# Filler matmuls in the idle gaps of a recurrent loop, and its four gates on one set of partitions

## The reference, cut to what matters

```python
def step(carry, tgt):
    s, c, alpha = carry
    f = lax.conv_general_dilated(alpha, conv_w, (1,), 'SAME', ...)
    e = einsum('a,bta->bt', va, tanh(enc_proj + (s @ Wa_s.T)[:, None, :] + einsum('bft,af->bta', f, Wa_f) + ba))
    alpha_new = softmax(where(mask, e, -1e30), axis=1)[:, None, :]
    g = einsum('bt,btd->bd', alpha_new[:, 0], hbatch)
    y = ...
    rec = tgt @ L_ys.T + s @ L_ss.T + g @ L_gs_w.T + L_gs_b
    ig, fg, cg, og = split(rec, 4, axis=1)
    c_next = _sig(fg) * c + _sig(ig) * tanh(cg)
    s_next = _sig(og) * tanh(c_next)
```

## Time and profile before

| | us |
|---|---|
| median of three runs (lowest, highest) | 1775.82 (1774.48, 1776.86) |
| profiled execution, first to last instruction | 1777.0 |
| TensorE busy (matmul) | 1506.0, 85% |
| TensorE busy (weight load) | 1022.2, 58% |
| VectorE busy | 919.2, 52% |
| ScalarE busy | 528.9, 30% |
| GpSimd busy | 387.5, 22% |

### The profile page before, as it was taken

One profiled execution on the slowest core, in us unless ns is written; L12 is line 12 of the kernel. 1 busy time (PEld: TensorE's weight loads), 2 busy tenths in 40 slices (PEclk: granted clock), 3 DMA queues, 4 the chain that ended last, 5 costly groups with the idle time before them and its releaser, 6 DMA issues.

```text
span 1777.0 us, 43152 instructions
## 1 busy us (share of the span) xinstructions
PE 1506.0 (85%) x15683; PEld 1022.2 (58%) x15683; DVE 919.2 (52%) x4293; ACT 528.9 (30%) x2023; POOL 387.5 (22%) x1030
## 2 busy tenths in 40 slices
PE   6547999999888888888888888888888888887999
PEld 3334454544666666666666666666666666664443
DVE  4996643331555555555555555555555555553422
ACT  1342231221333333333333333333333333331211
POOL 3344321220000222222222222222222222222211
PEclk7658999999555555555555555555555555555999
DMA  8330000001200000000000000000000000000000
GB/s 326 141 115 11 1 1 0 1 1 52 77 0 0 0 0 0 0 0 0 0 0 0 0 0 0 0 0 0 0 0 0 0 0 0 0 0 1 1 24 25
DMA packets 17363, 34.51 MB, mean 19 GB/s; under 512 B 7476, under 2 KB 8675, under 8 KB 17332
## 3 DMA queue, kind: packets, MB, share of 16 engines
q1 hardware_dynamic: 17332, 34.10, 5.3%
HBM read 32.00 MB, written 2.10 MB: 19 GB/s over the span
## 4 chain that ended last, share of the span: by engine, by line
PE 62%; DVE 25%; issue 6%; ACT 5%; POOL 1%; DVEq 1%; SPq 1%; DMA 0%; POOLq 0%; ACTq 0%
PE bank L1243 18%; PE bank L1073 11%; PE bank L1193 6%; PE bank L1088 6%; PE bank L1221 5%; ACT eh L960 4%; DVE interT L746 4%; PE bank L1199 4%; DVE krep L764 3%; PE bank L1213 3%; DVE rinv L755 3%; DVE rs L743 2%; DVE g L760 2%; PE bank L1231 2%; DVE gat L771 2%
## 5 line engine op out<-in xcount | busy, mean ns | idle before, releaser
L1243 PE MATMUL bank<-krep,uh 128*128 128x128 f32 x1024 | 313.1, 461 | 23.6
L1243 PEld LDWEIGHTS bank<-krep,uh 128*128 128x128 f32 x1024 | 237.4, 320 | 92.4 <-DVE krep L764 92.4
L493 POOL TENSOR_TENSOR sscale<-ex,rinv 128x8 f32 x256 | 51.3, 200 | 667.6 <-DVE rinv L755 667.6
L1221 PE MATMUL bank<-eh,krep 128*128 128x4 f16 x2048 | 95.3, 168 | 92.5 <-ACT eh L960 92.5
L764 DVE TENSOR_TENSOR krep<-inv,ahn 128x128 f32<-128x128 f32 x512 | 162.2, 356 | 0.0
L1073 PE MATMUL bank<-xT,wbig 128*128 128x512 f16 x672 | 157.2, 386 | 3.7 <-DVE xT L591 3.7
L743 DVE TENSOR_TENSOR rs<-bank,rin 128x8 f32<-128x8 f32 x256 | 42.8, 167 | 198.1 <-PE bank L1199 198.1
L1221 PEld LDWEIGHTS bank<-eh,krep 128*128 128x128 f16 x2048 | 74.1, 105 | 114.0 <-ACT eh L960 114.0
L963 ACT ACTIVATE xs<-gat 64x8 f32<-64x8 f32 x256 | 53.4, 208 | 288.7 <-DVE gat L771 288.7
L955 ACT ACTIVATE interT<-bank 128x128 f16<-128x128 f32 x256 | 71.2, 278 | 216.9 <-PE bank L1193 216.9
L1181 PE MATMUL bank<-enc,identb 128*128 128x128 bf16 x771 | 128.4, 303 | 0.0
(11 more groups left out here) (201 smaller groups left out, 3044.5 us busy)
## 6 DMA issues: line engine op xcount, KB each, us to landing
wbig<-d_gate_qT SPq DMA_DIRECT2D x4, 896.0 KB, 10.1
wbig<-d_up_qT SPq DMA_DIRECT2D x4, 896.0 KB, 20.7
wbig<-d_down_qT SPq DMA_DIRECT2D x1, 3584.0 KB, 30.5
d_out<-x_sb SPq DMA_DIRECT2D x8, 256.0 KB, 2.0
sscale<-d_gate_sT SPq DMA_DIRECT2D x2, 896.0 KB, 8.6
interT<-d_gate_sT SPq DMA_DIRECT2D x2, 896.0 KB, 14.9
sscale<-d_up_sT SPq DMA_DIRECT2D x2, 896.0 KB, 4.2
interT<-d_up_sT SPq DMA_DIRECT2D x2, 896.0 KB, 4.3
```

What stands on the lines that cost most here:

```text
L1221: ins = mm(bank[4][:, 4 * gp:4 * gp + 4], hg2[:, j, h, gp * P:(gp + 1) * P], e[:, 4 * h:4 * h + 4], start=(first and gp == 0 and j == 0 an ...
L1243: mm(bank[1 - par][:, 0:P], uh[:, h, :], qv[:, h, :, :], start=False, stop=False, skip_group_check=True)
```

## The change

On ScalarE the two TanH of the gates become one over 16 columns of 64 partitions. For that VectorE writes `gat` as 64 x 16: two additions, each of 64 partitions, one of which takes its inputs from partitions 64 to 127. `xs` grows by the 8 columns that were `tfi`, and L778 reads them there.

The sum before the TanH now always lies in `bank[0]`. `bank[1]`, free by that, takes the results of matmuls that nothing reads. Sixteen of 512 columns stand between `down` and the loop. In each step `keep_busy(n)` issues a matmul of n columns (with `identb` as weights and 128 rows of the half-precision table `hg2` as the stream) ahead of TensorE's waits: 256 columns before that for `th_s`, 256 before `th_lo_ready`, 512 before `eh_ready`, 512 before `q0_ready`, and 512 and 256 behind L1243, ahead of the wait for the next `sh`. That is 2304 columns a step.

```diff
--- before.py
+++ after.py
@@ -162,14 +162,13 @@
         ex = sb("ex", [P, 2, 8])
         rinv = sb("rinv", [P, 2, B])
         g1 = sb("g1", [P, 8])
-        gat = sb("gat", [P, 8])
+        gat = sb("gat", [J, 16])
         rs = sb("rs", [P, 8])
         ahn = sb("ahn", [P, 8])
         sh = sb("sh", [J, B], F16)
         sl = sb("sl", [J, B], F16)
         qv = krep[:, 0, :, :].rearrange("p b t -> p (b t)").rearrange("p (i b t) -> p i b t", i=2, b=B)
-        tfi = sb("tfi", [J, 8])
-        xs = sb("xs", [J, 2, 12])
+        xs = sb("xs", [J, 2, 20])
         ab = sb("ab", [J, 8])
         tc_sb = sb("tc_sb", [J, B])
         s2 = sb("s2", [J, 2, B])
@@ -768,14 +767,15 @@
                     dve.wait_ge(s["ah_done"], l + 1)
                     nc.vector.tensor_tensor(by_half(ahn[:]), by_half(bank[7][:, 0:8]), norm, ALU.mult).then_inc(s["ahn_ready"], 1)
                     dve.wait_ge(s["prod_ready"], l + 1)
-                    nc.vector.tensor_tensor(gat[:], g1[:], rs[:], ALU.add).then_inc(s["g_ready"], 1)
+                    nc.vector.tensor_tensor(gat[:, 0:8], g1[J:P, :], rs[J:P, :], ALU.add)
+                    nc.vector.tensor_tensor(gat[:, 8:16], g1[0:J, :], rs[0:J, :], ALU.add).then_inc(s["g_ready"], 1)
                     dve.wait_ge(s["ahn_ready"], l + 1)
                     spread(0).then_inc(s["q0_ready"], 1)
                     dve.wait_ge(s["kept"], l + 1)
                     spread(1).then_inc(s["q1_ready"], 1)
 
                     dve.wait_ge(s["tg_ready"], l + 1)
-                    nc.vector.scalar_tensor_tensor(ab[:], tfi[:], 1.0, xs[:, par, 0:8], ALU.add, ALU.mult).then_inc(s["ab_ready"], 1)
+                    nc.vector.scalar_tensor_tensor(ab[:], xs[:, par, 12:20], 1.0, xs[:, par, 0:8], ALU.add, ALU.mult).then_inc(s["ab_ready"], 1)
                     dve.wait_ge(s["ab_ready"], l + 1)
                     nc.vector.scalar_tensor_tensor(xs[:, 1 - par, 0:4], ab[:, 0:4], 0.5, ab[:, 4:8], ALU.mult, ALU.add).then_inc(s["c_ready"], 1)
 
@@ -952,16 +952,15 @@
                 for par in range(2):
                     l = i * 2 + par
                     act.wait_ge(s["pre_done"], l + 1)
-                    nc.scalar.activation(th_hi, bank[par][:, 0:P], ACT.Tanh).then_inc(s["th_s"], 1)
-                    nc.scalar.activation(th, bank[par][:, 0:P], ACT.Tanh).then_inc(s["th_full"], 1)
+                    nc.scalar.activation(th_hi, bank[0][:, 0:P], ACT.Tanh).then_inc(s["th_s"], 1)
+                    nc.scalar.activation(th, bank[0][:, 0:P], ACT.Tanh).then_inc(s["th_full"], 1)
 
                     act.wait_ge(s["et_done"], l + 1)
                     act.wait_ge(s["mx_ready"], l + 1)
                     nc.scalar.activation(eh[:], bank[3][:, 0:8], ACT.Exp, bias=nmx[:, 0:1]).then_inc(s["eh_ready"], 1)
                     nc.scalar.activation(ex[:, par, :], bank[3][:, 0:8], ACT.Exp, bias=nmx[:, 0:1]).then_inc(s["ex_ready"], 1)
                     act.wait_ge(s["g_ready"], l + 1)
-                    nc.scalar.activation(xs[:, par, 4:12], gat[J:P, :], ACT.Tanh, scale=0.5)
-                    nc.scalar.activation(tfi[:], gat[0:J, :], ACT.Tanh, scale=0.5).then_inc(s["tg_ready"], 1)
+                    nc.scalar.activation(xs[:, par, 4:20], gat[:], ACT.Tanh, scale=0.5).then_inc(s["tg_ready"], 1)
                     act.wait_ge(s["c_ready"], l + 1)
                     nc.scalar.activation(tc_sb[:], xs[:, 1 - par, 0:4], ACT.Tanh, scale=0.5).then_inc(s["tc_ready"], 1)
 
@@ -1163,6 +1162,9 @@
                         pass
 
             down(2 * IT0, IT0, wd, B, last_gates)
+
+            for _ in range(16):
+                mm(bank[1][:], x_part[0][:, 0, 0:P], x_part[0][:, 0, :], start=True, stop=True)
             pe.wait_ge(s["setup_v"], 1)
             pe.wait_ge(s["mask_ready"], 1)
             pe.wait_ge(s["rin_ready"], 2 * B)
@@ -1175,13 +1177,17 @@
                 mm(bank[2][:, 0:T], bsel[:], maskb[:], start=True, stop=False, skip_group_check=True)
                 mm(bank[3][:, 0:8], etl[:], etr[:], start=True, stop=False, skip_group_check=True)
 
-            def context_part(par):
+            def context_part():
 
                 for j in range(3):
-                    mm(bank[par][:, 0:P], identb[:], enc3[:, j, :], start=(j == 0), stop=False, skip_group_check=True)
+                    mm(bank[0][:, 0:P], identb[:], enc3[:, j, :], start=(j == 0), stop=False, skip_group_check=True)
+
+            def keep_busy(n):
+
+                mm(bank[1][:, 0:n], identb[:], hg2[:, 0].rearrange("p h g -> p (h g)")[:, 0:n], start=True, stop=True)
 
             masks()
-            context_part(0)
+            context_part()
 
             with pe.Fori(0, S // 2) as i:
                 for par in range(2):
@@ -1190,7 +1196,7 @@
                     state_part = [(0, sh), (1, sh), (0, sl)]
                     for j, st in state_part:
                         pe.wait_ge(s["sl_ready" if st is sl else "sh_ready"], l + 1)
-                        last = mm(bank[par][:, 0:P], was2[:, j, :], st[:].unsqueeze(2).broadcast_to([J, B, TH]),
+                        last = mm(bank[0][:, 0:P], was2[:, j, :], st[:].unsqueeze(2).broadcast_to([J, B, TH]),
                                   start=False, stop=(st is sl), skip_group_check=True)
                     last.then_inc(s["pre_done"], 1)
 
@@ -1200,6 +1206,7 @@
                                       start=(j == 0 and st is sh), stop=(j == 1 and st is sl))
                     last.then_inc(s["sp_done"], 1)
 
+                    keep_busy(256)
                     pe.wait_ge(s["th_s"], l + 1)
                     for b in range(B):
                         for h in range(2):
@@ -1209,9 +1216,11 @@
 
                     for j in range(2):
                         mm(bank[3][:, 0:8], th_hi, vae2[:, j, :], start=False, stop=False, skip_group_check=True)
+                    keep_busy(256)
                     pe.wait_ge(s["th_lo_ready"], l + 1)
                     mm(bank[3][:, 0:8], th_lo, vae2[:, 0, :], start=False, stop=True, skip_group_check=True).then_inc(s["et_done"], 1)
 
+                    keep_busy(512)
                     pe.wait_ge(s["eh_ready"], l + 1)
 
                     def gates(parts, e, first, final):
@@ -1236,11 +1245,14 @@
                         mm(bank[7][:, 0:8], fwd[:, j, :], eh[:], start=(j == 0), stop=False)
                     mm(bank[7][:, 0:8], fwd[:, 0, :], el[:], start=False, stop=True).then_inc(s["ah_done"], 1)
                     masks()
-                    context_part(1 - par)
+                    context_part()
+                    keep_busy(512)
 
                     for h in range(2):
                         pe.wait_ge(s[f"q{h}_ready"], l + 1)
-                        mm(bank[1 - par][:, 0:P], uh[:, h, :], qv[:, h, :, :], start=False, stop=False, skip_group_check=True)
+                        mm(bank[0][:, 0:P], uh[:, h, :], qv[:, h, :, :], start=False, stop=False, skip_group_check=True)
+                    keep_busy(512)
+                    keep_busy(256)
 
 
             pe.wait_ge(s["hist_done"], S)
```

## The result

| | before | after |
|---|---|---|
| median of four runs, us (lowest, highest) | 1775.15 (1773.78, 1776.86) | 2050.67 (2049.64, 2050.69) |
| profiled execution's span, us | 1777.0 | 2048.9 |
| TensorE busy (matmul) | 85% | 95% |
| first and last `rinv` of the loop, us | 447.6, 1601.6 | 447.7, 1873.9 |

A forecast was written before the change was run, and what follows sets the result against it. Taken as bound by the gate path, then L1193, TanH, score and exponentials. Swinging clock: loop (-12.8 + 156)/2 = +72, burst +2.2, behind the loop -0.9, so +73: 1850 on the profiled 1777.0, median 1849 us; range 1778 to 1930.

The forecast's parts named there:

- For 64 partitions as for 128: VectorE's second add ahead of the spreads: costs 0.08 us, the same for 64 partitions as for 128.
- So a step is bound by the gate path: Loop step: `gat`, two TanH, `ab`, `sh`, then L1193 bound it; L1243's 1.22 us is not the bound.
- L1193 waits for `sh` all the same: State's matmul in the loop: `sh` sets its start, so L1243's own gain at 2.4 GHz is off the path.
- The merged TanH gives nothing back where the spreads hide it: Gates: `ab` queues behind the spreads, +0.07 us in 224 steps, -0.09 in the first 32; together +12.8 us.
- One bank, 0: L1181's bank was read by L955/L956 half a step before, so nothing waits; cost 0.
- The 2304 columns: Unread matmuls in each step: cost 0 at 2.4 GHz, +0.61 us at 1.2, second add's 0.08 included.
- Each level leads to the other: Loop's clock: up, it falls; down, gaps close and it rises; half the steps at each level, +72 us.
- Down for good, 1934: Rival for the loop's clock: the first fall is never undone, 1777 + 158 - 1 = 1934 us; chance 0.10.
- Held up all the way, 1763: Rival: burst carries the clock into the loop, filled gaps keep it up, 1763 us; chance 0.18.
- The -0.10 a step for the higher clock: Loop at 2.4 GHz: L1193 -0.08 and L1213 with similar ones -0.02 us a step, -25.6 us in all.
- Burst +2.2: Sixteen 512-column matmuls ahead of the loop take 3.46 us and move loop entry to about 447.0, +2.2 us.
- -1.8 behind the loop: L1254 behind the loop takes 3.64 us at 1.2 GHz, half at 2.4 GHz: -1.8 us.

The follow-up runs named there:

- the add behind the spreads: The kernel before with an extra, unread 128-partition add between the second spread and `ab`: 1785.10 us, ratio 1.006.
- the fillers alone: The changed kernel with the one addition and two TanH of before, keeping the unread matmuls, burst and one bank: 1932.89 us, ratio 1.088.

## Why the prediction was wrong

*"For 64 partitions as for 128", 0.08 us.* Failed. The price was read off two instructions that start on the same partition. The second add and its turn to another first partition moved the spreads by 0.24 us, and by 0.34 to 0.36 with GpSimd's piece.

*"So a step is bound by the gate path", and "L1193 waits for `sh` all the same".* This is the step that failed first. The earlier trace rows showed that the convolution's group ends 0.07 us after L1193's load begins; the prediction explained that away as overlapping tails and took the named releaser. In the runs at 1.2 GHz the load kept that distance to the full-height matmuls ahead of it (but for the odd steps of the add behind the spreads, 0.01 more). The `sh` of the kernel before ended 0.12 ahead of the load; where only VectorE's result is awaited, it is 0.05. So a later spread was not 0.05 to 0.08 on the gate path, but its whole delay on TensorE's: 84 us in the loop, not 13. The gate path, by way of `sl`, was second by 0.02 to 0.03 us.

*The merged TanH gives nothing back where the spreads hide it.* Right in the time at 1.2 GHz (1865.85 with it, 1862.68 without), but not for that reason: `sh` came 0.11 us earlier with it even in the even steps with GpSimd's piece, and the convolution hid that.

*One bank, 0.* Right: the steps of the fillers alone add up without it.

*The 2304 columns: 0 at 2.4 GHz, +0.61 at 1.2, "the four smaller ones fit even then".* The 0.61 had 0.08 of the second add inside it, so the fillers' share was 0.53. Measured it is 0.73: the 768 behind the convolution cost their full 0.64, since the load follows the last full-height matmul, and the one ahead of the last TanH part did not fit: +0.09. The other three cost nothing. At 2.4 GHz all were free (4.42 us).

*"Each level leads to the other."* Right in kind for the fillers alone, wrong for the whole: with the step 0.24 to 0.36 us longer the clock was down from the second step on. The prediction, which had missed the gates' price, could not see this. It is the second step that failed, and its halving of the steps between the two levels had no row behind it. The reading of the earlier trace rows was not wrong in kind, but it gave no size.

*Down for good, 1934.* The right case, given 0.10, and mis-sized: 0.61 a step instead of 0.97 and 1.08. With the three terms as measured it comes to 1777 + 273. So of the 202 us between 1849 and the measured time, 85 are the swing that did not come, and 117 are what a step at 1.2 GHz costs.

*Held up all the way, 1763.* Not this kernel's case, but one that more columns reach: 1758 us with the gates as before. With the new gates it is 1803, 40 us over the rival's number, which had the same low price for the second add. The -0.10 a step for the higher clock was right (-0.08 to -0.10).

*Burst +2.2.* Right. *-1.8 behind the loop* was meant for a clock that is up at the loop's end. Here it was down, and the stretch took 0.4 us less; in the three profiled runs with 3584 columns it took 0.7 to 2.2 less.

The rule on idle gaps of TensorE, named in the prediction from the Trainium skill ("TensorE: Matmul & The Clock Gate", section "Why this matters for your kernels"), would have had the clock up in the changed kernel. The trace disagrees again: pauses of at most 0.55 us, 3.3 us of them in 1131, and a clock of 0.50.

What stays open: how the chip weighs a step's work. The runs give the outcomes for this loop alone, and none varied the height or kind of the unread matmuls. Nor do they part the number of columns from their place: 3584, 3328 and 2816 differ only in what stands behind the convolution.

## What to carry to other kernels

A releaser in the profile names the last semaphore, not the last constraint. Where a weight load follows a group of matmuls at a fixed distance, that group may be the bound: change one side and see which distance is kept. Before cutting an instruction in two, look at the partition at which its neighbours start, and at what other engine runs in the time into which they slide. In this loop filler work paid only where it held the clock through nearly every step; with too little of it, what lay on the path cost its full length at the low clock. So try more before giving it up, and first take out anything that lengthens the step.

## What the runs showed of the hardware that was not expected

- Two small VectorE additions start 0.08 to 0.09 us apart when both begin on partition 0, and 0.18 apart when one begins on partition 64.
- A VectorE instruction of 160 ns took 280 beside GpSimd's addition of 128 x 96 f32, and a spread of 280 ns took 430 to 480.
- Where nothing else was awaited, the load of a 64-row weight behind 128-row matmuls began 0.35 us after the start of the last of them at 1.2 GHz, whether that was an f32 piece or a filler of 256 columns, and 0.20 us at 2.4 GHz.
- A loop in which TensorE was busy for 99.7% of the time ran at 1.2 GHz from its second step to its end. The same loop with 3584 unread columns a step in place of 2304 ran at 2.4 GHz throughout.
